# A causal-attention and expert-MLP block: all score blocks transposed by VectorE and moved per group, rope products on GpSimd

## What is computed

```python
q = (xn @ wq.T)                      # 16 heads x 64
lat = xn @ w_kv_down.T               # 64 latent features
k, v = lat @ w_k_up.T, lat @ w_v_up.T
q = q * cos + rotate_half(q) * sin
k = k * cos + rotate_half(k) * sin
scores = q @ k.T / 8 + causal
out = softmax(scores) @ v
x = x + out @ wo.T + ffn(xn)         # 16 experts, top 4 of 2 groups of 4, and a shared one
```

## Time and profile before

| | us |
|---|---|
| median of 3 runs | 577.34 (574.35 to 577.7) |
| the profiled execution, whole | 571.87 |
| its span in the profile | 570.1 |
| TensorE busy in the span | 514.0 |
| VectorE busy | 445.5 |
| ScalarE busy | 366.2 |
| GpSimd busy | 223.8 |
| first VectorE turn of a group begins at | 128.6 |
| last VectorE turn begins at | 536.0 |

### The profile page before, as it was taken

The page is one execution under the profiler, slowest core; times in us unless marked ns, Lnnn a source line. Parts: engine busy times, 40 slices in busy tenths (PEclk is TensorE's granted clock), DMA queues, the critical chain, the costliest instruction groups (busy, mean ns, idle before and its releaser), DMA issues.

```text
span 570.1 us, 13180 instructions
## 1 busy us (share of the span) xinstructions
PE 514.0 (90%) x4651; PEld 363.7 (64%) x4658; DVE 445.5 (78%) x921; ACT 366.2 (64%) x972; POOL 223.8 (39%) x327
## 2 busy tenths in 40 slices
PE   2899999986899998999999999999999997999854
PEld 2567777753567675767667766667676675766643
DVE  5696546359989998999899999989998997778700
ACT  2563222355567876787787777877777877678722
POOL 2014204002345453545544654645455444322232
PEclk9899999998899999999999999999999999999987
DMA  9400005102687768777676877687786868876761
GB/s 277 134 2 1 1 0 114 35 2 53 146 201 194 168 156 193 191 166 189 161 198 162 209 187 181 159 201 192 189 198 164 206 152 186 180 187 158 164 153 37
DMA packets 41617, 83.26 MB, mean 146 GB/s; under 512 B 13632, under 2 KB 20688, under 8 KB 41424
## 3 DMA queue, kind: packets, MB, share of 16 engines
q1 hardware_dynamic: 34512, 66.29, 47.9%
q0 software_dynamic: 4480, 14.68, 11.4%
q10 hardware_dynamic: 2560, 1.45, 0.9%
HBM read 5.84 MB, written 1.05 MB: 12 GB/s over the span
## 4 chain that ended last, share of the span: by engine, by line
PE 82%; issue 7%; DVE 4%; ACT 3%; DMA 1%; DVEq 0%; POOLq 0%; SPq 0%; POOL 0%; ACTq 0%
PE ps L382 26%; PE ps L428 25%; PE ps L328 5%; PE ps L456 5%; PE ps L474 5%; PE ps L411 4%; PE ps L441 4%; PE ps L330 2%; PE ps L331 1%; DMA acc<-x 1%; PE ps L344 1%; PE ps L458 1%; PE ps L363 1%; DVE prob L777 1%; ACT prob L598 1%
## 5 line engine op out<-in xcount | busy, mean ns | idle before, releaser
L777 DVE CUSTOM_DVE_ANT_0 prob<-ps,mask 128x1024 f32<-128x1024 f32 (+7 forms) x256 | 181.0, 754 | 39.1 <-PE ps L382 37.1
L598 ACT ACTIVATE prob<-prob,negmax 128x1024 f32<-128x1024 f32 (+7 forms) x256 | 196.2, 776 | 15.5 <-DVE negmax L777 15.5
L382 PE MATMUL ps<-qk 64*128 64x512 f32 (+3 forms) x768 | 161.0, 524 | 15.3 <-DVE negmax L777 14.5
L862 POOL TENSOR_TENSOR acc<-acc,scaled 128x256 f32<-128x256 f32 x128 | 93.4, 730 | 148.5 <-ACT scaled L501 143.3
L790 DVE STREAM_TRANSPOSE zig<-prob 128x896 f32<-128x896 f32 x128 | 134.1, 1086 | 2.3 <-DMA fastT<-zig 2.2
L428 PE MATMUL ps<-fastT,lat 128*64 128x128 f32 x1792 | 115.0, 281 | 15.3 <-issue 12.5
L428 PEld LDWEIGHTS ps<-fastT,lat 128*64 128x64 f32 x1792 | 99.5, 139 | 32.5 <-issue 25.4
L382 PEld LDWEIGHTS ps<-qk 64*128 64x128 f32 x768 | 64.1, 188 | 72.1 <-issue 41.2
L853 POOL TENSOR_TENSOR roped<-prod 128x256 f32<-128x256 f32 x64 | 46.7, 730 | 152.6 <-DVE prod L667 152.6
L501 ACT ACTIVATE scaled<-ps,rden 128x128 f32<-128x128 f32 x256 | 73.0, 368 | 40.9 <-PE ps L441 40.9
L667 DVE TENSOR_TENSOR prod<-ps,rope 128x1024 f32<-128x1024 f32 x64 | 78.2, 1221 | 3.2 <-PE ps L328 1.6
(11 more groups left out here) (117 smaller groups left out, 459.6 us busy)
## 6 DMA issues: line engine op xcount, KB each, us to landing
fastT<-zig SPq DMA_DIRECT2D x512, 112.0 KB, 2.3
qk<-roped POOLq DMA_DIRECT2D x56, 256.0 KB, 4.8
qk<-roped SPq DMA_DIRECT2D x8, 256.0 KB, 4.8
acc<-x SPq DMA_DIRECT2D x2, 512.0 KB, 5.5
rope<-c_rope SPq DMA_DIRECT2D x1, 1024.0 KB, 10.7
out<-acc SPq DMA_DIRECT2D x2, 512.0 KB, 3.5
wq_raw<-wq ACTq DMA_DIRECT2D x1, 512.0 KB, 6.6
wo_raw<-wo ACTq DMA_DIRECT2D x1, 512.0 KB, 7.7
```

The costliest lines, as they stand in the source:

```text
L382: mm = nc.tensor.matmul(to, qk[p][half, 0, rows], qk[p][half, 1, lo:hi], start=True, stop=True)
L598: nc.scalar.activation(row, row, ACT.Exp, bias=negmax[:, col:col + 1], scale=-1.0, accum_out=den[:, col:col + 1]).then_inc(exp_done, 1)
L777: nc.vector.tensor_tensor_reduce(row_sb(k, r), row_ps(k, r), mask[:, S - width:], -1.0, 3e38, ALU.add, ALU.min, accum_out=negmax[:, col:co ...
L862: nc.gpsimd.tensor_tensor(rows, rows, scaled[k % 2][:, a], ALU.add).then_inc(ad_done, 1)
```

## The change

`LAG` goes from 4 to 3, and `FAST`, `SLOW`, `SLOTS` are gone: `turn_slow` and `copy_slow` are dropped and VectorE's `turn_fast` turns all nine blocks (128 x 1152 in place of 128 x 896). The exchange is made group by group: four DMAs, each from 32 partitions of `zig` to all 128 of `fastT` (288 KB each), with rings of three `zig` and four `fastT`. A piece of partition 32c + p lands in partition 4p + c, so the latent is permuted once in the same way (`latp`). The rope product leaves VectorE in the loop: ScalarE copies the piece from PSUM bank 4 to `raw` (`copy_rope`), and GpSimd multiplies (`multiply`, 128 x 1024) ahead of its `rotate`. GpSimd's `stack` calls stand elsewhere, and the second half of the output goes out in four stores.

```diff
-LAG = 4
-SLOTS = LAG + 1
+LAG = 3
-FAST = 7
-SLOW = QB + 1 - FAST
+BLKS = QB + 1
 def rope_bank(e):
-    return 6 + e % 2 if e < LATER else 7
+    return 6 + e % 2 if e < LATER else 4
-SWAPS = 16 * 16
+SWAPS = 4 * 16
+RING4, RING3 = 4, 3
...
-        zig = [sb(f"zig{s}", [P, 4, 2, 2, FAST, 32], f32) for s in range(2)]
-        fastT = [sb(f"fastT{s}", [P, 4, 2, 2, FAST, 32], f32) for s in range(2)]
-        slowT = [sb(f"slowT{s}", [P, 2, SLOW, P], f32) for s in range(SLOTS)]
+        zig = [sb(f"zig{s}", [P, 4, 2, BLKS, 32], f32) for s in range(RING3)]
+        fastT = [sb(f"fastT{s}", [P, 4, 2, BLKS, 32], f32) for s in range(RING4)]
+        raw = [sb(f"raw{s}", [P, 2, QW], f32) for s in range(2)]
...
-            def exchange(j):
-                s = j % 2
-                sp.wait_ge(zig_done, 4 * j + 4)
-                if j >= 2:
-                    sp.wait_ge(pv_done, 2 * (j - 1))
-                for turn_ in range(4):
-                    for qi in range(4):
-                        ki = (qi + turn_) % 4
-                        sp.dma_start(fastT[s][32 * ki:32 * ki + 32, qi],
-                                     zig[s][32 * qi:32 * qi + 32, ki]).then_inc(in_fast[s], 16)
+            def exchange(k):
+                s = k % RING4
+                sp.wait_ge(zig_done, 2 * k + 2)
+                if k >= RING4:
+                    sp.wait_ge(pv_done, k - RING4 + 1)
+                for qi in range(4):
+                    sp.dma_start(fastT[s][:, qi], zig[k % RING3][32 * qi:32 * qi + 32]).then_inc(in_fast[s], 16)
+
+            sp.wait_ge(first_act, 11)
+            for c in range(4):
+                sp.dma_start(latp[bass.ds(c, 32, step=4)], lat[32 * c:32 * c + 32]).then_inc(in_latp, 16)
...
-            def turn_slow(k):
...
             def products(k):
-                s, first = k // 2 % 2, QB * (unit_of(k) // QUADS)
-                pe.wait_ge(slow_act, k + 1)
-                pe.wait_ge(in_fast[s], SWAPS * (k // 4 + 1))
+                s, first = k % RING4, QB * (unit_of(k) // QUADS)
+                pe.wait_ge(in_fast[s], SWAPS * (k // RING4 + 1))
...
                 for e in pieces_at(k):
-                    if k >= LAG + 1:
-                        pe.wait_ge(scaled_done, 4 * (k - LAG - 1) + 2)
-                    pe.wait_ge(rope_dve, e)
+                    if k == 0:
+                        pe.wait_ge(added, 2 * BLOCKS)
+                    else:
+                        pe.wait_ge(rope_act, k)
                     rotary(e)
...
-            def copy_slow(k):
...
+            def copy_rope(k):
+                act.wait_ge(rope_pe, k + LATER + 1)
+                if k >= 2:
+                    act.wait_ge(multiplied, k - 1)
+                copy(raw[k % 2][:], ps[:, rope_bank(k + LATER), :].rearrange("p (t n) -> p t n", t=2)).then_inc(rope_act, 1)
...
+            def multiply(e):
+                pool.wait_ge(rope_act, e - LATER + 1)
+                pool.wait_ge(rot_done, e - 1)
+                nc.gpsimd.tensor_tensor(prod[:, e % 2], raw[(e - LATER) % 2][:].unsqueeze(2).broadcast_to([P, 2, 2, QW]),
+                                        rope[:, :, quarter(e)].unsqueeze(1).broadcast_to([P, 2, 2, QW]),
+                                        ALU.mult).then_inc(multiplied, 1)
...
-                for e in pieces_at(k):
-                    rotate(e)
-                n = unit_of(k + 4)
-                if (k + 4) % 8 == 0 and 1 <= n < UNITS:
+                n = unit_of(k + 3)
+                if (k + 3) % 8 == 0 and 1 <= n < UNITS:
                     pool.wait_ge(rot_done, PIECES * (n + 1))
                     stack(n, 0)
-                n = unit_of(k + 1)
-                if (k + 1) % 8 == 0 and 1 <= n < UNITS:
+                n = unit_of(k - 1)
+                if (k - 1) % 8 == 0 and 1 <= n < UNITS:
                     pool.wait_ge(short_done, 2 * 8 * n)
                     stack(n, 1)
+                for e in pieces_at(k):
+                    multiply(e)
+                    rotate(e)
```

More of the change, by code:

```diff
@@ L104, in block_kernel @@
         lat = sb("lat", [P, TILES, LAT], f32)
+        latp = sb("latp", [P, TILES, LAT], f32)
         mix = sb("mix", [P, HEADS // 2, P], f32)
@@ L196, in block_kernel @@
             sem, "long_done short_done max_done exp_done rden_done".split())
[L197 to L200, removed]
+        zig_done, pv_done, o_done, proj_pe, scaled_done, ad_done, multiplied = map(
+            sem, "zig_done pv_done o_done proj_pe scaled_done ad_done multiplied".split())
+        rope_pe, rope_dve, rope_act, rot_done, stored = map(
+            sem, "rope_pe rope_dve rope_act rot_done stored".split())
+        in_fast = [sem(f"in_fast{s}") for s in range(RING4)]
+        in_latp = sem("in_latp")
         in_first = [sem("in_first0"), sem("in_first1")]
@@ L248, in _ @@
             out_tiles = out.rearrange("b (i p) d -> p (b i) d", p=P)
-            for k in range(-1, GRPS):
-                if k >= 0 and k % 2:
-                    exchange(k // 2)
+            for k in range(GRPS):
+                exchange(k)
                 if k == GRPS // 2 + LAG + 3:
@@ L254, in _ @@
                     sp.dma_start(out_tiles[:, 0:QB, :], acc[:, 0:QB, :]).then_inc(stored, 16)
-            sp.wait_ge(ad_done, 2 * GRPS)
-            sp.dma_start(out_tiles[:, QB:, :], acc[:, QB:, :]).then_inc(stored, 16)
+            for k in range(GRPS - 4, GRPS):
+                sp.wait_ge(ad_done, 2 * (k + 1))
+                lower_i, gap = SHORT[k % 4], LONG[k % 4] - SHORT[k % 4]
+                rows = bass.ds(QB + lower_i, 2, step=gap)
+                sp.dma_start(out_tiles[:, rows, :], acc[:, rows, :]).then_inc(stored, 16)
             for p in range(PAIRS):
                 sp.wait_ge(in_qk[p], STACK * (UNITS - 1))
-            sp.wait_ge(stored, 32)
+            sp.wait_ge(stored, 16 * 5)
         @block.tensor
@@ L400, in short_scores @@
                 scores(k, 2, 0)
[L402 to L413 removed]
             def products(k):
[L416 to L418 removed]
+                s, first = k % RING4, QB * (unit_of(k) // QUADS)
+                pe.wait_ge(in_fast[s], SWAPS * (k // RING4 + 1))
+                if k == 0:
+                    pe.wait_ge(in_latp, 64)
                 if k:
@@ L423, in products @@
                         to = ps[HD * a:HD * a + HD, 6, (r // 2) * P:(r // 2 + 1) * P]
-                        if at < FAST:
-                            probs = fastT[s][:, :, k % 2, a, at, :]
-                        else:
-                            probs = slowT[k % SLOTS][:, a, at - FAST, :]
-                        last = nc.tensor.matmul(to, lat[:, first + kb, :], probs, start=(at == 0),
-                                                stop=(at == QB))
+                        last = nc.tensor.matmul(to, latp[:, first + kb, :], fastT[s][:, :, a, at, :],
+                                                start=(at == 0), stop=(at == QB))
                 last.then_inc(pv_done, 1)
@@ L434, in project @@
                 pe.wait_ge(o_done, k + 1)
-                pe.wait_ge(rope_dve, min(k + LAG + 1 + LATER, PIECES * UNITS))
-                if k:
+                if not k:
+                    pe.wait_ge(rope_dve, LATER)
+                    pe.wait_ge(added, 2 * BLOCKS)
+                else:
                     pe.wait_ge(scaled_done, 4 * k)
@@ L843, in rotate @@
                 n, z = e // PIECES, e % PIECES
-                pool.wait_ge(rope_dve, e + 1)
+                if e < LATER:
+                    pool.wait_ge(rope_dve, e + 1)
+                else:
+                    pool.wait_ge(multiplied, e - LATER + 1)
                 if n >= 2 and z == 0:
```

27 lines of the change are left out of this document (6 added, 21 removed).

## The result

| | before | changed |
|---|---|---|
| median, us | 577.52 (574.35 to 579.87, 4 runs) | 595.67 (595.28 to 598.23, 4 runs) |
| ratio to before | | 1.0337, 95% interval 1.0289 to 1.0386 |
| the profiled execution, whole / span | 571.87 / 570.1 | 598.23 / 596.3 |
| TensorE, VectorE, ScalarE, GpSimd busy | 514.0, 445.5, 366.2, 223.8 | 489.3, 417.6, 361.1, 346.8 |

The account below looks back on a forecast made before the run. Exchange the bound: start 130.7, 424 us of carrying and 1.7 landing give 556.4; products' 2.1 and 8.5 after give span 567.0, 3 us less than now, so median 577.34 becomes 574 us; range 553 to 595.

Parts of the forecast that it names:

- the stacks' term: GpSimd's stacks issued later: loss 0 to 7 us, value 3, if TensorE bounds; nothing if the exchange does.
- The landing: Stack DMAs before the scores: the last is issued some 2 us after the first and lands 4.8 us later.
- The issue: GpSimd's stack calls: they move one and two iterations later, data there about when the first pair's scores want it.
- TensorE's gaps: Between long and short scores, without transposes: 1.27, 1.19, 1.03 and 0.87 us, a gain of 3 us.
- the operations: GpSimd's 1024-wide product 2.35 us (2.92 the other price); VectorE's longer turn at most 1.396 us.
- GpSimd is not full: Rival: GpSimd's multiply becomes the bound if a product takes 3.0 us or more; 581 or 597 us, chance 0.12.
- my first rival: TensorE stays the bound and exchange waits go: 557 us, between 552 and 564, chance 0.28.
- the rate: Exchange on the DMA engines: 207 GB/s alone, bounds 197 and 213; 233 GB/s together with a stack.
- spread badly: Rival: wide exchange writes spread badly over the DMA engines; some 900 us, or 683 at three quarters rate; chance 0.06.

Follow-up runs that it names:

- The variant that comes nearest to being bound by the exchange: Changed kernel, stacks at old places, rotary ahead of short_scores, one more rope piece made ahead, first pair's stack issued one iteration earlier: 552.22 us, ratio 0.9563.

## Why the prediction was wrong

I forecast 574 us with the exchange as the bound, and a range of 553 to 595. It was 595.67, above the range.

**The step that failed is the stacks' term**: "the loss at 0 to 7 us, value 3, where TensorE is the bound; nothing where the exchange is". It measured 23.4 us between two kernels that differ in nothing else. Three things were wrong in it.

- *The landing.* I took 4.8 us after the last issue from the earlier trace rows. That is the median of single DMAs, at the load of before. What scores wait for is the last of four that share the engines with the exchange: 7.4 to 9.4 us in the 14 places of the changed kernel. The figure stood in my own text: a stack holds the engines for 7 us. A landing must be taken from a stretch with the load that the change makes, and for the last of the DMAs.
- *The issue.* I counted iterations. The order of instructions showed the stack behind `add_head`, and I did not follow that back to the `project` it hangs from, ScalarE's queue and the rope product. That path takes from 380.82 to 392.02, 11.2 us. It leaves TensorE 398.63 - 392.02 = 6.6 us of work to cover 9.0.
- *"Nothing where the exchange is the bound."* That holds only if the exchange goes on while TensorE waits. It does for some microseconds, but VectorE's turns hang from the scores, so the supply of pieces stops with them: SP's queue waits 133.2 us for `zig` in the changed kernel and 104.1 with both stacks back. From 200 to 500 us the DMA share is 0.87 there and 0.92 with the stacks back, and the exchange was not the bound at all.

The two profiled executions, changed and with both stacks back, are 596.3 - 567.7 = 28.6 us apart. TensorE's waits for stacks are 33.2 - 13.3 = 19.9 us more, those for the exchange 1.1 more, those for the maximum 2.2 less, and its busy time is 489.3 - 479.3 = 10.0 more though it does the same work. That sums to 28.8. Of the 10.0, 7.0 are in the scores (L387, 168.2 and 161.2 us); the last section shows where most of them lie.

**Right: TensorE's gaps.** With the transposes gone they were to be 1.27, 1.19, 1.03 and 0.87 us. In the changed kernel with both stacks back the chain has long and short scores of the narrowest group at

```profile
407.35 1.33 PE ps L387 x8
...
409.55 1.13 PE ps L387 x4
```

that is 409.55 - 408.68 = 0.87. The wider groups of the same chain have 1.26, 1.14 and 1.00 (from 389.41, 396.09 and 402.65 to 390.67, 397.23 and 403.65). Removing 0.60 us of transposes in 64 groups was forecast at 3 us, and the kernel of before without them shows no gain that can be measured (interval 0.9969 to 1.0067).

**Right: the operations.** The product is 2.362 us where I said 2.35, so GpSimd is not full. It is still 14% of the chain, since its product and additions stand ahead of a stack's issue, and that I had not counted. The turn is 1.354 where I said at most 1.396.

**Right in time, not in cause: 574.** With its stacks back the change gives 572.28. But `products` waits there for 3.0 us only, at 212 to 222 GB/s and shares of 0.90 to 0.93. TensorE is 54% of its chain, with 47.5 us of waits for the maximum and 13.3 for stacks. So that the two numbers are near each other is luck. The sum of my first rival is the one that fits: it had 557 with 3 us for stacks in it, 554 without, and with the measured 13.3 and 3.0 us it comes to 570. With half the exchange and stacks at the old places, where neither transfer is waited for, the time is 551.32.

**Mis-sized: the rate.** I took 207 GB/s for exchanges alone and 233 beside a stack, with bounds of 197 and 213. The variant that comes nearest to being bound by the exchange (552.22 us) moves 222 to 240 GB/s in windows of 50 us, stacks included, and 224 from 130 to 530 us; mine make 90.2 MB / 424 us = 213 as a mean over the same mixture. At 224 the 90.2 MB take 403 us, 21 less, and my own sum would have given 553 by this estimate. So the exchange as a bound stands near the 552 us of that variant, not at 574. How much of this is the wider write and how much the steady supply isn't separated. The Trainium skill, "SBUF — State Buffer", section "Door 1: The DMA port swizzle", gives an asymptote of 218 GB/s for partitions 0 to 31. The mean of 224 is near it, but 240 GB/s in one window (stacks included, which read 32 partitions as well) is above it.

**The rest.** The wide write did not spread badly, and slower came by none of the rivals I had listed for it. The rival that was missing hides in my own text, in the sentence that prices the stacks at 3 us.

## What to carry to other kernels

Moving a transfer's issue later is priced by its deadline: follow the issue back to the engine that will wait for it, take the landing of the *last* DMA at the load that the change itself makes, and compare with the work that lies between. An engine that is freed of filler work gets nothing back until the wait under the filler is filled or removed, and then it comes sooner to the next landing: from 572 to 566 and 552 us each step met the next wait. Take an edit that bundles parts apart: three of these gain 27 us together, and two lose 46.

## What the runs showed of the hardware

**A stall can cost more than its length.** Where TensorE had been idle for 2.56 us before the long scores, they took 2.63 us; after 1.73 us of idle time they took 2.01. Windows of 1 us of the changed kernel show why (the clock is the third value from the right):

```profile
401.50:402.50 1.00, 1.00 (x6) 0.45 (x4) 0.00 (x0) 0.00 (x0) 0.23 (x1) 0.92 0.83 205
402.50:403.50 1.00, 1.00 (x4) 0.40 (x2) 0.00 (x0) 0.00 (x0) 0.00 (x0) 0.50 0.90 134
...
405.50:406.50 1.00, 1.00 (x7) 0.75 (x6) 1.00 (x5) 1.00 (x3) 0.87 (x2) 0.87 0.76 131
```

The granted clock fell from 1.00 (2.4 GHz) to 0.50 (1.2 GHz) about a microsecond after the engine had resumed, and was back some 3 us later. The length of the stall does not decide it alone. In the changed kernel scores that began at 230.92, behind 1.96 us of idle time, took 3.02 us, and with both stacks back scores behind 2.60 us took 2.01, at a clock of 1.00; in the timeline of the latter:

```profile
387.40 1.99 PE L387 MATMUL ps<-qk 64*128 64x512 f32 x8 [2.60 <-DMA qk<-roped]
```

In the changed kernel the long scores behind 7 of the 14 stacks took 2.39 to 3.63 us in place of 2.01; with both stacks back that is one of seven. Over 2.01 us each, the seven sum to 7.5 us and the one to 1.5. The difference, 6.0, is most of the 7.0 us above, and no term of my sum had it.

**A stack beside a full exchange.** The last of a stack's four DMAs lands 7.40 to 9.44 us after its issue at 1.18 MB a group (14 places of the changed kernel's chain), and 6.94 to 8.79 at 0.92 MB (12 places of the kernel with only the exchange, `LAG`, the last stores and the stacks' place changed). With both stacks back at 1.18 MB the longest is 10.20 us, in a stretch with the share at 1.00 and 227 GB/s; with `rotary` in the gap as well it is 11.45. At 0.59 MB three places have 5.62 to 6.75.
